# Two attentions over keys: shifted scores are transposed before the exponential, and the exponential takes the place of ScalarE's copy out of PSUM

## What is computed

```python
def _L1_xattn_ref(hidden_states, context, attention_mask, q_w, q_b, k_w, k_b, v_w, v_b):
    ...
    scores = jnp.einsum('bhqd,bhkd->bhqk', q, k) / jnp.sqrt(jnp.float32(HD))
    mask = (attention_mask > 0)[:, None, None, :]
    scores = jnp.where(mask, -jnp.inf, scores)
    probs = jax.nn.softmax(scores, axis=-1)
    ctx = jnp.einsum('bhqk,bhkd->bhqd', probs, v)
...
def _L3_xattn_ref(q, kv, q_w, q_b, k_w, k_b, v_w, v_b, o_w, o_b):
    ...
    attn = jnp.einsum('bhqc,bhkc->bhqk', qh, kh) * SCALE
    attn = jax.nn.softmax(attn, axis=-1)
    out = jnp.einsum('bhqk,bhkc->bhqc', attn, vh)
    out = out.transpose(0, 2, 1, 3).reshape(b, nq, h * c)
    return out @ o_w.T + o_b
```

## Time and profile before

| | |
|---|---|
| median of 3 runs | 1575.79 us (1572.86 to 1581.02) |
| profiled execution, span from first to last instruction | 1577.4 us |
| mean granted TensorE clock | 0.927 of full speed |
| busy: PE, PEld | 1300.2 us (82%), 1110.4 us (70%) |
| busy: DVE, ACT, POOL | 1024.4 (65%), 938.3 (59%), 593.1 (38%) |
| attention 1, first to last exponential | 606.2 to 716.6 us |
| attention 3, first to last exponential | 1221.7 to 1373.9 us |

### The profile page before, as it was taken

How to read it: one execution, slowest core, us unless ns; L and a number is a source line. 1 busy time by engine, 2 the same in 40 slices (tenths; PEclk the granted TensorE clock), 3 DMA queues, 4 the chain that set the end, 5 groups by cost and what they waited for, 6 DMA issues and landing times. The chain is left out here.

```text
span 1577.4 us, 42313 instructions
## 1 busy us (share of the span) xinstructions
PE 1300.2 (82%) x16531; PEld 1110.4 (70%) x16555; DVE 1024.4 (65%) x2551; ACT 938.3 (59%) x2128; POOL 593.1 (38%) x576
## 2 busy tenths in 40 slices
PE   7999999978999988993479874977743888888994
PEld 5888999856888886882256553966741767688994
DVE  7798997834534336997789978433326788763445
ACT  4666666533444446996346434644536998735884
POOL 3334333310000003341468731777750024443662
PEclk9999999999999998996679887999986999988997
DMA  6411100089990002320000010111121001002335
GB/s 193 177 32 29 38 20 3 2 138 145 167 116 1 1 1 81 118 73 1 14 15 22 9 55 11 48 48 48 50 93 70 16 26 36 30 32 59 97 89 179
DMA packets 140982, 93.81 MB, mean 59 GB/s; under 512 B 55456, under 2 KB 126752, under 8 KB 140272
## 3 DMA queue, kind: packets, MB, share of 16 engines
q1 hardware_dynamic: 131920, 72.79, 21.6%
q0 software_dynamic: 8864, 18.30, 3.6%
HBM read 51.06 MB, written 39.99 MB: 58 GB/s over the span
## 5 line engine op out<-in xcount | busy, mean ns | idle before, releaser
L439 POOL TENSOR_TENSOR wide_probs<-wide_probs,wide_key_mask 128x512 f32<-128x512 f32 x44 | 64.6, 1487 | 119.8 <-ACT wide_probs L623 119.8
L1723 POOL DMA_INDIRECT moe_x_rows<-moe_rows,moe_source x71 | 80.6, 1136 | 72.4 <-DVE moe_source L1822 51.0
L916 POOL TENSOR_TENSOR attn_col_bd<-attn_col_t,group_mask_sb 128x1024 f32<-128x1024 f32 x32 | 60.6, 1894 | 106.3 <-ACT attn_row_t L1131 106.3
L886 POOL MEMSET attn_v_bd<- 128x576 f32 x2 | 1.2, 614 | 263.3 <-POOLq L168 263.3
L2428 DVE TENSOR_TENSOR moe_hidden<-banks,moe_gate 128x256 f32<-128x256 f32 x103 | 43.2, 423 | 82.9 <-ACT moe_gate L2636 80.7
L3253 ACT ACTIVATE moe_router<-banks,moe_rb_sb 128x512 f32<-128x512 f32 x64 | 41.4, 688 | 88.3 <-PE banks L3359 66.4
L2093 POOL DMA_INDIRECT moe_rows<-moe_xhat,moe_slot x64 | 61.9, 967 | 68.8 <-DVE moe_slot L2393 49.7
L2265 POOL DMA_INDIRECT moe_results<-moe_y_rows,moe_x_rows x71 | 68.0, 957 | 51.4 <-issue 29.6
L1006 DVE TENSOR_REDUCE attn_top<-banks 128x32 f32<-128x2048 f32 x32 | 73.0, 2282 | 21.9 <-PE banks L1192 21.8
L1729 POOL DMA_INDIRECT moe_results<-moe_y_rows,moe_dest x71 | 73.3, 1033 | 21.6 <-issue 20.7
L1160 ACT ACTIVATE attn_probs<-attn_probs 128x1024 f32<-128x1024 f32 x64 | 65.7, 1052 | 25.1 <-DVE attn_probs L1035 23.8
(11 more groups left out here) (460 smaller groups left out, 4297.5 us busy)
## 6 DMA issues: line engine op xcount, KB each, us to landing
moe_rows<-route_empty_sb SPq DMA_DIRECT2D x8, 2624.0 KB, 23.1
attn_ctx<-in_ctx_t SPq DMA_DIRECT2D x48, 128.0 KB, 2.1
moe_x_rows<-moe_rows SPq DMA_DIRECT2D x71, 66.0 KB, 1.9
moe_pack_sb<-in_moe_pack SPq DMA_DIRECT2D x8, 578.0 KB, 4.1
moe_w_sb<-in_moe_w SPq DMA_DIRECT2D x2, 2048.0 KB, 7.4
moe_hot<-moe_results SPq DMA_DIRECT2D x16, 256.0 KB, 5.7
moe_until_back<-moe_results SPq DMA_DIRECT2D x16, 256.0 KB, 5.6
moe_pack_sb<-in_moe_pack SPq DMA_DIRECT2D x9, 384.0 KB, 4.8
```

What stands on the lines that cost most here:

```text
L439: nc.gpsimd.tensor_tensor(some, some, keys, ALU.mult).then_inc(masked, 1)
L916: nc.gpsimd.tensor_tensor(col_bd[:], col_t[u.parity][:].unsqueeze(1).to_broadcast(shape), w["group_mask"][:].unsqueeze(2).to_broadcast(sha ...
L1723: nc.gpsimd.indirect_dma_start(x_rows[s % GATHERS][:], None, rows, bass.IndirectOffsetOnAxis(ap=source[:, s:s + 1], axis=0)).then_inc(gath ...
```

## The change

In attentions 1 and 3 `probs_back` transposes the shifted scores as DVE leaves them, and `take_probs` makes the exponential where it made a copy: it reads the bank in PSUM and writes `probs_t`. The two exponentials in place and the semaphore `exped` go. PE then waits for DVE's `shifted`. In attention 3 one wait is new: for duo 4 and later, the first `probs_back` waits for `take_rows` of the step before ahead of its second bank; until now ACT's exponential, queued behind `take_rows`, had implied that. Attention 2 keeps its exponential; the `return` after the values is reached in attention 1 alone.

```diff
@@ narrow_attention, scalar: take_probs
-                            nc.scalar.copy(probs_t[t][:, 4 * n:4 * n + 4].rearrange("p f q -> p (f q)"), pt_bank[n][:]
-                                           ).then_inc(pt_taken, 1)
+                            nc.scalar.activation(probs_t[t][:, 4 * n:4 * n + 4].rearrange("p f q -> p (f q)"), pt_bank[n][:],
+                                                 ACT.Exp, scale=scale).then_inc(pt_taken, 1)
@@ narrow_attention, scalar: after the values, over_keys
                             ins.then_inc(v_taken, 1)
+                            return
                         for t in range(2):
                             act.wait_ge(shifted, b.at(2, 1 + t))
@@ narrow_attention, tensor: probs_back
-                    pe.wait_ge(exped, u.at(2, 1 + t))
+                    pe.wait_ge(shifted, u.at(2, 1 + t))
@@ attention_into_experts, scalar: end of a step
-                    if inside(b):
-                        act.wait_ge(shifted, b + 1)
-                        for t in range(2):
-                            part = probs[b % 2][:, t].rearrange("p h k -> p (h k)")
-                            nc.scalar.activation(part, part, ACT.Exp, scale=scale).then_inc(exped, 1)
@@ attention_into_experts, tensor: probs_back
-                    pe.wait_ge(exped, 2 * u + 1 + t)
+                    pe.wait_ge(shifted, u + 1)
                     for n in range(2):
                         if t == 1:
                             pe.wait_ge(pt_taken, 4 * u + 1 + n)
                         elif u >= 1:
                             pe.wait_ge(pt_taken, 4 * u - 1 + n)
+                        if t == 0 and n == 1 and u >= 4:
+                            pe.wait_ge(rt_taken, u - 3)
```

More of the change, by code:

```diff
@@ L2143, in attention_into_experts @@
         projected, qk_taken, biased = sem("projected"), sem("qk_taken"), sem("biased")
-        scored, topped, shifted, exped = sem("scored"), sem("topped"), sem("shifted"), sem("exped")
+        scored, topped, shifted = sem("scored"), sem("topped"), sem("shifted")
         v_made, v_taken = sem("v_made"), sem("v_taken")
```

## The result

Over 20 runs of each kernel on one chip the changed kernel takes 1581.26 us (1576.64 to 1588.16) and the kernel before 1576.03 (1572.3 to 1581.02): a ratio of 1.0026, interval 1.0014 to 1.0038. (The ratio is estimated from all the runs; the two medians alone would give 1.0033.) It is 2 to 6 us slower, a loss inside the 0.5% that the forecast calls "same". But a gain of 3.9 us was forecast, and 1581.26 lies above the forecast's range of 1565.5 to 1578. So the two spans don't show the loss; the stages do.

The account below looks back on a forecast made before the run. PE's own work bounds attention 1, an ACT-PE loop attention 3. Terms -1.7 (end of attention 1), -2.2 (long steps), -0.3 (short steps), +0.2 (tiles), +0.1 (table load) give -3.9: 1575.8 to 1571.9 us; range 1565.5 to 1578.

Parts of the forecast that it names:

- The clock falls elsewhere: Rival: attention 3's moved work meets clock falls differently, 4 us either way of the forecast, 1568 or 1576; chance 0.12.
- End of attention 1, -1.7: Last duos of attention 1: transposes no longer wait for the exponential, so the last product begins earlier; gain 1.7 us.
- Full steps of attention 1, 0: Attention 1's full steps stay at PE's own 7.12 us, so removing ACT's exponentials gains 0 there.
- shorter than 7.1: Sign of being wrong: attention 1's step falls below 7.1 us, where 7.12 was expected to stay.
- PE already waits for nothing: Reason given for 0 gain in attention 1's full steps: PE's work is unchanged and has no waits to remove.
- ACT was the limit: Rival: PE's full row hides waits, so attention steps shrink to DVE's share, 0.83 us each in attention 1; 1552; chance 0.12.
- Long steps of attention 3, -0.28 each: Attention 3's long steps: 0.28 of the 0.35 us wait for `heads_t` is saved; eight steps give 2.2 us.
- Short steps: Attention 3's short steps: 0.10 of the 0.17 us wait is saved; three steps give 0.3 us.
- Tiles and table load: Attention 3: exponentials out of PSUM at 600 ns cost 0.2 us over 28 tiles; the table load moved to step 3 costs 0.1.
- estimate with a drain: Alternative by the skill page: a drain of about 1.38 us at the table switch makes the gain 1.4 us smaller, 1573.2.
- PE's new wait for `take_rows`: Attention 3, ahead of the second bank: some 1.5 us of slack, so cost 0.

Follow-up runs that it names:

- the slower groups: First three of four experiment groups, each with its own runs of the kernel before, which takes 1634.58, 1634.38 and 1645.67 us there.
- idle matmuls: Unread matmuls added in attention 3 where PE waits (4 of 128x256, 1 of 128x512): changed kernel 1632.54 us, 0.9978 to before; kernel before 1632.58 us, 0.9980.
- late links: Changed kernel with DVE's two small next-stage normalization instructions put behind its shifts from step 12 of attention 1: 1638.93 us, 1.0022 to before.
- the old pace: Changed kernel with three ACT exponentials of other data, result unread, where attention 3's old ones stood: 1636.59 us, 1.0015 to before.
- the last group's two kernels: Kernel before and changed kernel, each with unread matmuls in attention 3 and DVE's small instructions behind its shifts in attention 1: 0.9968 and 0.9947 to before.

## Why the prediction was wrong

**The step that failed** is the rival "The clock falls elsewhere". It made the clock a noise of 4 us either way around the forecast with a chance of 0.12, and the sum counted nothing for it. In fact the change lowers the clock of attention 3 (0.92 to 0.88 in the runs of the result, 0.87 to 0.84 on the mean of the slower groups), and the stage is 5.1 and 4.6 us longer, although each undisturbed step is shorter. The rows for suspecting it stood in the trace: PE's share of a long step is 87%, its clock fell there twice, and these two steps cost 1.24 and 1.03 us. The changed kernel has three such steps more, and two of its five cost over 2.8 us; that outweighs the whole gain. That the clock is what takes the gain back is shown: idle matmuls are worth 9.9 us in the changed kernel and 2.1 in the kernel before, and with them and late links in both kernels the change gains 4.8. That the falls hang on the step's pace rests on one trace with the old pace. Why a step of 9.94 us meets them more often than one of 10.32 stays open: PE is busy for 88% of an undisturbed step after and for 87% before, so the share over a step doesn't explain it.

**End of attention 1, -1.7.** The transposes of the last duo begin at 713.76 and the product at 715.20, where 714.2 and 715.6 were forecast:

```profile
713.76 1.09 PE L1222 MATMUL banks<-ident_sb,attn_probs 128*128 128x128 f32 x8
...
715.20 1.11 PE L1285 MATMUL banks<-attn_v_bd,attn_probs_t 128*64 128x18 f32 x32 [0.34 <-ACT attn_probs_t L1121]
```

Counted from the last `xhat` of the stage (697.60, before 698.29) the product comes 17.60 us behind it, before 19.02: 1.4 us gained, and no wait of the transposes is left. The rest of the stage's gain comes from its full steps.

**Full steps of attention 1, 0.** They are 7.05 us and not 7.12, over twelve steps 0.9 us, and "shorter than 7.1" was one of the prediction's own signs of being wrong. "PE already waits for nothing" was not quite so. PE's weight loads before:

```profile
645.55 0.91 PEld L1221 LDWEIGHTS banks<-ident_sb,attn_probs 128*128 128x128 f32 x8
646.51 0.30 PEld L1248 LDWEIGHTS banks<-attn_ctx,attn_wk_sb 128*128 128x128 f32 x2
```

and after:

```profile
643.77 0.91 PEld L1222 LDWEIGHTS banks<-ident_sb,attn_probs 128*128 128x128 f32 x8
644.65 0.30 PEld L1249 LDWEIGHTS banks<-attn_ctx,attn_wk_sb 128*128 128x128 f32 x2
```

The projection of the keys follows the transposes by 0.96 us before and by 0.88 after: 0.08 us in which it waited, most likely for ACT's copy of `x_t`, queued behind the exponentials. The modelled ends of the matmuls covered it, as the rival "ACT was the limit" had feared, at a tenth of the size given there (0.08 us a step and not 0.83). With the end this makes attention 1 117.2 to 115.0 us in traces without the collision and at clock 1.00 (117.2, 117.2, 117.3 against 115.0, 115.1, 115.0, 115.0). The collision itself the prediction didn't see: it never laid POOL's instructions beside DVE's.

**Long steps of attention 3, -0.28 each.** They gained 0.38: the output projection comes 0.87 us behind the transposes (1264.80, 1265.67), as computed, and the projections of the keys 0.45 behind it (1266.12); before, 0.55 (1311.91, 1312.46). The sum had only the first of the two. Short steps: 8.59 for 8.78, -0.19 and not -0.10.

**Tiles and table load.** The tile's price and the load's own duration were right, the load's place in the loop was not. Timeline of ACT after:

```profile
1217.82 1.28 ACT L2656 ACT_TABLE_LOAD   x1
1219.11 1.09 ACT L2656 ACTIVATE moe_until_back<-banks 128x512 f32<-128x512 f32 x2
1220.08 1.94 ACT L2667 ACTIVATE moe_until_back<-banks,attn_group_bias,group_mask_sb 128x256 f32<-128x256 f32 x4
```

A tile costs 2 ns more than the copy in attention 1 (595 for 593) and nothing more in attention 3 (603 for 604); the load takes 1.28 us, with its successor right behind it (1219.11) and no drain of its own; the step with it is 9.67 us after and 9.24 before, 0.4 us and not 0.1. (The prediction's estimate with a drain should read 1573.3: 1571.9 and 1.38.) PE's new wait for `take_rows` shows nowhere.

**What stays open.** The change in attention 1 alone measured 1.0020 without late links and 0.9993 with them, on two chips. Its attention 1 took 116.6 and 115.0 us, where the old one took 117.2 and 120.5 in the same groups, so it should have gained in both, and neither interval decides. Attention 3 loses 4.6 or 5.1 us, and attention 1 gains some 2.2 (117.2 to 115.0, with the collision's 1.6 and 1.7 on either side): 2 to 3 us of loss, where the measured one is 4.1 (2.2 to 6.0).

## What to carry to other kernels

Where PE has gaps in a stage, its granted clock is a term of the sum and not a noise: read how many stretches of low clock the stage has, what one costs, and what some more or fewer would make of the forecast, before trusting a saving of some tenths of a microsecond a step. A step shortened on another engine may pay only once PE's gaps are filled: the same change lost 0.26% in the kernel as it was, and with idle matmuls and late links in both kernels it gained 0.2 to 0.3%. What a repair is worth is counted from the same kernel without it. Look also at what begins at the same moment on DVE and POOL; a shift of 0.1 us decides whether a tiny instruction takes 0.17 us or 1.84.

## What the runs showed of the hardware

A DVE instruction with two inputs in SBUF (128x16) that began with, or 0.08 us behind, a POOL instruction of 1.89 us took until that one's end, 1.84 to 1.92 us; DVE's shift, which reads PSUM, took its usual 2.36 us beside it. The Trainium skill ("SBUF — State Buffer", SBUF: two separate sides) describes a pair of ports that DVE and GpSimd lock for a whole instruction, a DVE operation with two SBUF inputs among those concerned. The traces agree, and add that with starts equal to 0.01 us either outcome occurs: DVE got through in two traces, where POOL's instruction took 1.93 and 1.94 us in the place of 1.89, and waited in two others. A small DVE instruction with one input in SBUF was held too: in the kernel before L218 began 0.85 us behind a spread at 604.24, took 1.07 us and ended with it.

PE's clock fell right behind the part of a step in which PE waited for 0.32 and 0.56 us, although in undisturbed steps with the same waits PE was busy for 8.75 of 10 us at clock 1.00, and five idle matmuls a step, 1.0 us of PE, left no fall at all in the 100 us from 1250 in the last group's two kernels.
